# An adapter and LoRA kernel: x of the first two batches loaded in halves, and three more early chunks multiplied in high and low parts

## The chip, the cores and the metric

The kernel runs on one core of one Trainium2 chip. The metric is the device time of one execution in microseconds (us). Its engines are TensorE (PE, matmuls; PEld is its weight load), VectorE (DVE), ScalarE (ACT), GpSimd (POOL) and SyncE (SP), which here only issues transfers. ACTq and SPq are the instruction queues from which an engine issues transfers.

## The reference

Eight batches of x, each of 128 rows by 512 columns. Each batch picks one of 16 adapters (512 by 512) by its id; the result then goes through a base layer and a routed LoRA of 8 experts of rank 16:

```python
y = einsum('bij,bkj->bik', x, weight[adapter_ids])
q = y[:, 107:127].mean(axis=1)
routing = softmax(q @ router_W.T + router_b)
base = y @ W.T + b
t = einsum('bsd,erd->bser', y, A)
lora = einsum('bser,eor,be->bso', t, B, routing) * 2
out = x + base + lora
```

All data is float32.

## The kernel before

The contraction of 512 is cut into four chunks of 128 (C = 4; HALF = 2 chunks). For a batch, y gathers in one PSUM bank over four chunks: x's chunk (128 by 128) is the stationary operand, the adapter's chunk (128 by 512) the moving one. y is then copied to SBUF by ScalarE (copy_y, L265), transposed by TensorE (transpose_y, L544; for batches 4 to 7 VectorE's turn, L406, and transfers do this), and two batches together, a pair g, are multiplied with A and W (products, L552) and with the routed B (lora, L569). VectorE finishes the output (finish, L443) with the bias and x, and SyncE stores it.

A product is made in one of two ways. Raw (y_raw, L511) multiplies the float32 operands as they are; the trace shows two passes for one chunk. Split makes three matmuls of type float32r out of one: ScalarE casts an operand to its high part (hi_...), VectorE subtracts that from the operand to get the low part (lo_...), and TensorE adds high by high, high by low and low by high. Before, batches 0 and 2 are all raw, batch 1 is raw in chunks 0 and 1 and split in chunks 2 and 3 (y1_split, L520, fed by hi_x1, L289, and hi_wc1, L293, and by lo_x1, L380, and lo_wc1, L385), and batches 3 to 7 are split (y_split, L531, fed by hi_x, hi_wc, lo_x, lo_wc).

The order of work is written out by hand, one instruction list for each engine, with semaphores between them. An engine takes its list strictly in order, so an instruction that waits holds all behind it. SyncE issues the loads in the order in which they are listed (L198 to L217): the two halves of adapter 0, x of batch 1, the halves of adapter 1, x of batch 2, and so on; the halves of an adapter are 512 KB each, x of a batch 256 KB. x of batch 0 alone is issued by ScalarE (L311), before its first cast. Adapters are addressed by ids that SyncE reads first (L179).

TensorE's list (L582 to L659) begins with 11 matmuls on zeros, then batch 0, chunks 0 and 1 of batch 1, the transposes of batch 0, chunks 2 and 3 of batch 1, and batch 2 with the transposes of batch 1 after its first chunk. Later the pairs' products alternate with the batches to come. VectorE's list (L449 to L505) ends in a loop over pairs g = 1, 2, 3: the router's parts, half 0 of adapter 2g + 3, the turn of batch 2g + 2, half 1 of that adapter, logits, routing, the low part of t, the next turn, x and adapter 2g + 4, the low parts of yT, and the outputs.

Of the kernel before, what the change touches and what calls it, by code (L numbers as in the profile page):

```python
# [5 lines left out]
P = 128  # L6
# [9 lines left out]
CONSTS = 44  # L16


def adapter_lora_kernel(nc, xT0, xT, ids, wcT, rest0, rest1, rest2, rest3, out):


    _, _, _, C, S = xT.shape
    ALONE = xT0.shape[0]
    PAIRS = xT.shape[0] + ALONE // 2
    B = 2 * PAIRS
    D = C * P
# [7 lines left out]
    RAW = 3  # L34
    WARM_UPS = 11
    ON_PE = 4
    T = 32
    NT = P // T
    assert S == P and C == 4 and B == 8

    with ExitStack() as ctx:
# [6 lines left out]
        def sem(name):  # L48
            return ctx.enter_context(nc.semaphore(name))
# [48 lines left out]
        az_raw = [rest_raw[:, n:n + D] for n in az_at]  # L98
        b_raw = rest_raw[:, FIRST + D:SECOND]

        x_in = [sem(f"x{b}_in") for b in range(ALONE)] + [sem(f"x_pair{g}_in") for g in range(ALONE // 2, PAIRS)]
        wc_in = [[sem(f"wc{b}_in{n}") for n in range(2)] for b in range(B)]
        rest_in = [sem(f"rest{n}_in") for n in range(4)]
        stored = [sem(f"stored{g}") for g in range(PAIRS - 1)]
# [13 lines left out]
        xT_lo_ready = sem("xT_lo_ready")  # L118
        wc_hi_ready = sem("wc_hi_ready")
        wc_lo_ready = sem("wc_lo_ready")  # L120
        x1_hi_ready = sem("x1_hi_ready")
        x1_lo_ready = sem("x1_lo_ready")
        wc1_hi_ready = sem("wc1_hi_ready")
        wc1_lo_ready = sem("wc1_lo_ready")

        y_done = sem("y_done")
        y_copied = sem("y_copied")
# [22 lines left out]
        def flat(t):  # L150
            return t.rearrange("p c s -> p (c s)")
# [4 lines left out]
        def half_of(h):  # L156
            return slice(HALF * h, HALF * (h + 1))

        def x_arrived(b):
            return x_in[b if b < ALONE else b // 2 + ALONE // 2]  # L160

# [15 lines left out]
        @block.sync  # L177
        def _(sp):
            _, a = nc.values_load_multi_w_load_instructions(  # L179
                ids, engines=[mybir.EngineType.SP], min_val=0, max_val=NADAPT - 1,  # L180
                skip_runtime_bounds_check_because="each load of an adapter checks its own address against the table")

            def load_wc(b, h):
                sp.dma_start(wc_raw[:, b, half_of(h), :].rearrange("p c o -> p (c o)"),  # L184
                             wcT[bass.ds(a[b], 1), h].rearrange("a p c o -> (a p) (c o)"))\
                    .then_inc(wc_in[b][h], 16)

            def load_x(b):
                sp.dma_start(flat(xT_raw[:, b]), xT0[b]).then_inc(x_arrived(b), 16)

            def load_x_pair(g):
                sp.dma_start(xT_raw[:, 2 * g:2 * g + 2].rearrange("p b c s -> p (b c s)"),
                             xT[g - ALONE // 2].rearrange("p b c s -> p (b c s)")).then_inc(x_arrived(2 * g), 16)

            def load_rest(n, rest, cols):
                sp.dma_start(rest_raw[:, cols], rest).then_inc(rest_in[n], 16)

            load_wc(0, 0)  # L198
            load_wc(0, 1)
            load_x(1)  # L200
            load_wc(1, 0)
            load_wc(1, 1)
            load_x(2)
            load_wc(2, 0)
            load_rest(0, rest0, slice(0, CONSTS + D))
            load_wc(2, 1)
            load_x(3)
            load_rest(1, rest1, slice(CONSTS + D, FIRST))
            load_rest(2, rest2, slice(FIRST, SECOND))
            load_rest(3, rest3, slice(SECOND, THIRD))  # L210
            load_wc(3, 0)
            load_wc(3, 1)
            for g in range(ALONE // 2, PAIRS):
                load_x_pair(g)
                for b in (2 * g, 2 * g + 1):
                    load_wc(b, 0)
                    load_wc(b, 1)  # L217

            def store(g):
                for c in range(C):  # L220
                    sp.wait_ge(o_ready[c], g + 1)
                sp.dma_start(out[g], o_sb[:, g].rearrange("p c b s -> p c (b s)")).then_inc(stored[g], 16)

            for g in range(1, PAIRS - 1):
                store(g - 1)
                move_blocks(sp, 2 * g + 2)
                move_blocks(sp, 2 * g + 3, range(NT if g == 1 else HALF))
            store(PAIRS - 2)
            for c in range(C):
                sp.wait_ge(o_ready[c], PAIRS)  # L230
                sp.dma_start(out[PAIRS - 1, :, c], o_sb[:, PAIRS - 1, c].rearrange("p b s -> p (b s)"))\
                    .then_inc(last_stored[c], 16)
            for g in range(PAIRS - 1):
                sp.wait_ge(stored[g], 16)
            for c in range(C):
                sp.wait_ge(last_stored[c], 16)
# [17 lines left out]
        def _(act):  # L254
# [31 lines left out]
                    copy(flat(wc_hi[b % 2][:, half_of(h), :]), flat(wc_raw[:, b, half_of(h), :]))\  # L286
                        .then_inc(wc_hi_ready, 1)

            def hi_x1():  # L289
                act.wait_ge(x_arrived(1), 16)  # L290
                copy(flat(xT_hi[1][:, HALF:]), flat(xT_raw[:, 1, HALF:])).then_inc(x1_hi_ready, 1)  # L291

            def hi_wc1(c):  # L293
                act.wait_ge(wc_in[1][1], 16)
                copy(wc_hi[1][:, c, :], wc_raw[:, 1, c, :]).then_inc(wc1_hi_ready, 1)

            def exponent(g):
                act.wait_ge(nmax_ready, g + 1)
# [9 lines left out]
                                         scale=rout[:, i:i + 1]).then_inc(tsT_hi_ready, 1)  # L308

            act.wait_ge(ident_ready, 1)  # L310
            act.dma_start(flat(xT_raw[:, 0]), xT0[0]).then_inc(x_arrived(0), 16)  # L311
            act.wait_ge(warm_ready, 1)
            nc.scalar.activation(junk[:], warm[:, 0:1], ACT.Exp)

            hi_x1()
            copy_y(0, ps_y)
            for c in range(HALF, C):
                hi_wc1(c)
            hi_yT(0)
            copy_y(1, ps_o[3])  # L320
            hi_az(0)
# [33 lines left out]
        def _(dve):  # L355
# [21 lines left out]
                    tt(flat(wc_lo[b % 2][:, part_h, :]), flat(wc_raw[:, b, part_h, :]),  # L377
                       flat(wc_hi[b % 2][:, part_h, :]).bitcast(F32), ALU.subtract).then_inc(wc_lo_ready, 1)

            def lo_x1():  # L380
                dve.wait_ge(x1_hi_ready, 1)
                tt(flat(xT_lo[1][:, HALF:]), flat(xT_raw[:, 1, HALF:]), flat(xT_hi[1][:, HALF:]).bitcast(F32),  # L382
                   ALU.subtract).then_inc(x1_lo_ready, 1)

            def lo_wc1(c):  # L385
                dve.wait_ge(wc1_hi_ready, c - HALF + 1)
                tt(wc_lo[1][:, c, :], wc_raw[:, 1, c, :], wc_hi[1][:, c, :].bitcast(F32), ALU.subtract)\
                    .then_inc(wc1_lo_ready, 1)

            def lo_yT(b):  # L390
                pair, i = b // 2 % 2, b % 2
# [55 lines left out]
                    .then_inc(o_ready[c], 1)  # L447

            nc.vector.memset(warm[:], 0.0).then_inc(warm_ready, 1)  # L449
            lo_x1()  # L450
            for c in range(HALF, C):
                lo_wc1(c)
            lo_yT(0)
            lo_az(0)
            lo_yT(1)
# [12 lines left out]
            lo_wc(3)  # L468
            lo_az(4)
            for b in range(2):  # L470
                dve.wait_ge(x_arrived(b), 16)
            finish(0, 0)
            finish(0, 1)
            lo_x(4)
# [5 lines left out]
            for g in range(1, PAIRS):  # L480
                ahead = 2 * g + 2 < B
                router_parts(g)
                if ahead:
                    lo_wc(2 * g + 3, (0,))
                    turn(2 * g + 2)
                    lo_wc(2 * g + 3, (1,))
                logits(g)
                routing(g)
                lo_tsT(g)
                if ahead:  # L490
                    turn(2 * g + 3)
                if 2 * g + 4 < B:
                    lo_x(2 * g + 4)
                    lo_wc(2 * g + 4)
                if ahead:
                    lo_yT(2 * g + 2)
                for c in range(3):
                    finish(g, c)
                if ahead:
                    lo_yT(2 * g + 3)  # L500
                if 2 * g + 4 < B:
                    lo_x(2 * g + 5)
                if g < PAIRS - 1:
                    finish(g, 3)
# [3 lines left out]
        def _(pe):  # L508
            mm = nc.tensor.matmul

            def y_raw(b, c, bank):  # L511
                if c == 0:
                    pe.wait_ge(x_arrived(b), 16)
                if c % HALF == 0:
                    pe.wait_ge(wc_in[b][c // HALF], 16)
                last = mm(bank[:], xT_raw[:, b, c, :], wc_raw[:, b, c, :], start=(c == 0), stop=(c == C - 1))  # L516
                if c == C - 1:
                    last.then_inc(y_done, 1)

            def y1_split(c, bank):  # L520
                if c == HALF:
                    pe.wait_ge(x1_lo_ready, 1)
                pe.wait_ge(wc1_hi_ready, c - HALF + 1)
                mm(bank[:], xT_hi[1][:, c, :], wc_hi[1][:, c, :], start=False, stop=False)
                mm(bank[:], xT_lo[1][:, c, :], wc_hi[1][:, c, :], start=False, stop=False)
                pe.wait_ge(wc1_lo_ready, c - HALF + 1)
                last = mm(bank[:], xT_hi[1][:, c, :], wc_lo[1][:, c, :], start=False, stop=(c == C - 1))
                if c == C - 1:
                    last.then_inc(y_done, 1)

# [52 lines left out]
            for _ in range(WARM_UPS):  # L583
                mm(ps_l[:], warm[:, 0:P], warm[:], start=True, stop=True)  # L584

            for c in range(C):
                y_raw(0, c, ps_y)
            for c in range(HALF):
                y_raw(1, c, ps_o[3])
            pe.wait_ge(ident_ready, 1)  # L590
            transpose_y(0)
            for c in range(HALF, C):
                y1_split(c, ps_o[3])
            for c in range(C):
                y_raw(2, c, ps_y)
                if c == 0:
# [111 lines left out]
```

## Time and profile before

| | us |
|---|---|
| median of 3 runs | 72.85 (72.40 to 73.01) |
| the profiled execution | 72.17 |
| its span in the trace | 70.5 |
| TensorE busy | 65.9 (94%) |
| VectorE busy | 43.0 (61%) |
| ScalarE busy | 30.5 (43%) |

The profile is of one execution. The span runs from its first to its last instruction. Busy time of TensorE counts overlapping matmuls once; a matmul's record is longer than its step, since matmuls are pipelined, so the step from one record's start to the next is what one costs in a full queue. The granted TensorE clock is 1.0 of full speed in all 40 slices.

### The profile page before, as it was taken

The numbers are of one execution on the slowest core, as the hardware profiler recorded it, in microseconds if no ns is written. First come the engines' busy times: TensorE is split into PE (matmuls) and PEld (weight loads), VectorE is DVE, ScalarE is ACT, GpSimd is POOL, SyncE is SP. The second block draws the span as 40 slices with busy tenths as digits, with TensorE's granted clock in tenths as the row PEclk, the third lists the DMA queues.
The fourth block names the chain that finished last, engine by engine and source line by source line (L and its number), as shares of the span: only waits on it lengthen the run. The fifth ranks groups of instructions, "written<-read, shape, count | busy, mean of one in ns | idle before, by whom it ended". The sixth has DMA issues, their size and how long they took to land.

```text
span 70.5 us, 1142 instructions
## 1 busy us (share of the span) xinstructions
PE 65.9 (94%) x409; PEld 53.9 (76%) x409; DVE 43.0 (61%) x105; ACT 30.5 (43%) x62; POOL 1.2 (2%) x10
## 2 busy tenths in 40 slices
PE   2999989999999999999999999999999999999930
PEld 1332425743999988988988999888699999999920
DVE  1000022938999999779955999699554298250720
ACT  0800055487898993593036997300330330330000
POOL 5000000000000000000000000000000000000000
PEclk9999999999999999999999999999999999999999
DMA  0489999999999999999824014007230600600242
GB/s 0 112 265 384 358 387 409 417 405 414 409 407 412 407 409 405 409 409 402 333 64 104 9 42 107 0 0 298 47 88 19 151 3 9 284 14 0 69 154 74
DMA packets 7062, 15.30 MB, mean 217 GB/s; under 512 B 784, under 2 KB 3344, under 8 KB 7056
## 3 DMA queue, kind: packets, MB, share of 16 engines
q1 hardware_dynamic: 6624, 14.84, 56.2%
q10 hardware_dynamic: 432, 0.39, 2.1%
q8 instruction: 3, 0.05, 0.3%
q14 instruction: 3, 0.02, 0.1%
HBM read 12.08 MB, written 2.10 MB: 201 GB/s over the span
## 4 chain that ended last, share of the span: by engine, by line
PE 81%; DMA 8%; SPq 4%; issue 1%; DVE 1%
PE ps_o L556 32%; PE ps_t L556 8%; PE ps_o L573 8%; DMA wc_raw<-in_wcT_dram 8%; PE ps_y L516 5%; PE ps_y L539 4%; PE ps_y L538 4%; PE ps_y L540 4%; PE ps_yT L538 3%; PE ps_o L516 3%; PE ps_yT L540 3%; PE ps_yT L539 3%; PE ps_yT L549 3%; SPq L179 2%; SPq L184 1%
## 5 line engine op out<-in xcount | busy, mean ns | idle before, releaser
L556 PE MATMUL ps_o<-yT_hi,az_hi 128*128 128x256 f32 x64 | 18.1, 283 | 0.0
L556 PE MATMUL ps_o<-yT_lo,az_hi 128*128 128x256 f32 x64 | 17.8, 279 | 0.0
L556 PE MATMUL ps_o<-yT_hi,az_lo 128*128 128x256 f32 x64 | 17.8, 279 | 0.0
L556 PEld LDWEIGHTS ps_o<-yT_hi,az_hi 128*128 128x128 f32 x64 | 12.0, 188 | 0.1
L556 PEld LDWEIGHTS ps_o<-yT_hi,az_lo 128*128 128x128 f32 x64 | 12.0, 188 | 0.1
L556 PEld LDWEIGHTS ps_o<-yT_lo,az_hi 128*128 128x128 f32 x64 | 12.0, 188 | 0.0
L377 DVE TENSOR_TENSOR wc_lo<-wc_raw,wc_hi 128x1024 fp32r<-128x1024 f32 x10 | 11.9, 1211 | 0.1
L286 ACT CAST wc_hi<-wc_raw 128x1024 fp32r<-128x1024 f32 x10 | 10.0, 1052 | 0.0
L445 DVE SCALAR_TENSOR_TENSOR o_sb<-ps_o,rest_raw,xT_raw 128x256 f32<-128x256 f32 x16 | 7.1, 478 | 3.1 <-PE ps_o L573 3.1
L300 ACT ACTIVATE expd<-logit,nmax 128x8 f32<-128x8 f32 x8 | 2.3, 293 | 12.8 <-DVE nmax L427 12.8
L516 PE MATMUL ps_y<-wc_raw,xT_raw 128*128 128x512 f32 x16 | 7.4, 597 | 0.2 <-DMA wc_raw<-in_wcT_dram 0.2
L584 PE MATMUL ps_l<-warm 128*128 128x512 bf16 x11 | 4.9, 632 | 1.3 <-DVE warm L449 1.3
L516 PEld LDWEIGHTS ps_y<-wc_raw,xT_raw 128*128 128x128 f32 x16 | 2.9, 190 | 3.5 <-issue 2.9
L382 DVE TENSOR_TENSOR xT_lo<-xT_raw,xT_hi 128x256 fp32r<-128x256 f32 x1 | 0.4, 424 | 8.0 <-ACT xT_hi L291 8.0
L539 PE MATMUL ps_y<-wc_lo,xT_hi 128*128 128x512 f32 x12 | 4.7, 391 | 0.0
L538 PE MATMUL ps_y<-wc_hi,xT_hi 128*128 128x512 f32 x12 | 4.7, 391 | 0.0
L540 PE MATMUL ps_y<-wc_hi,xT_lo 128*128 128x512 f32 x12 | 4.7, 389 | 0.0
L399 DVE TENSOR_TENSOR yT_lo<-yT_raw,yT_hi 128x512 fp32r<-128x512 f32 x4 | 2.8, 689 | 3.0 <-ACT yT_hi L276 3.0
L556 PE MATMUL ps_t<-yT_hi,az_hi 128*128 128x256 f32 x16 | 4.6, 285 | 0.0
L573 PE MATMUL ps_o<-tsT_hi,b_hi 128*128 128x256 f32 x16 | 4.6, 284 | 0.0
L276 ACT CAST yT_hi<-yT_raw 128x512 fp32r<-128x512 f32 x4 | 2.5, 624 | 4.7 <-issue 2.9
L573 PE MATMUL ps_o<-tsT_lo,b_hi 128*128 128x256 f32 x16 | 4.5, 283 | 0.0
(71 smaller groups left out, 111.9 us busy)
## 6 DMA issues: line engine op xcount, KB each, us to landing
wc_raw<-in_wcT_dram SPq DMA_DIRECT2D x16, 512.0 KB, 12.1
out_dram<-o_sb SPq DMA_DIRECT2D x3, 512.0 KB, 3.7
rest_raw<-in_rest_dram SPq DMA_DIRECT2D x2, 512.0 KB, 9.5
xT_raw<-in_xT_dram SPq DMA_DIRECT2D x2, 512.0 KB, 14.3
yT_raw<-y_turn SPq DMA_DIRECT2D x14, 64.0 KB, 2.1
xT_raw<-in_xT_dram SPq DMA_DIRECT2D x3, 256.0 KB, 6.7
out_dram<-o_sb SPq DMA_DIRECT2D x4, 128.0 KB, 1.9
rest_raw<-in_rest_dram SPq DMA_DIRECT2D x1, 278.0 KB, 7.6
```

What stands on the lines that cost most here:

```text
L276: copy(yT_hi[b // 2 % 2][:, :, b % 2, :].rearrange("p c (n s) -> p c n s", n=NT), yT_raw[b % 2].rearrange("p n c s -> p c n s")).then_inc( ...
L286: copy(flat(wc_hi[b % 2][:, half_of(h), :]), flat(wc_raw[:, b, half_of(h), :]))\
L377: tt(flat(wc_lo[b % 2][:, part_h, :]), flat(wc_raw[:, b, part_h, :]), flat(wc_hi[b % 2][:, part_h, :]).bitcast(F32), ALU.subtract).then_in ...
L399: tt(yT_lo[pair][:, :, i, :].rearrange("p c (n s) -> p c n s", n=NT), yT_raw[i].rearrange("p n c s -> p c n s"), yT_hi[pair][:, :, i, :].r ...
L445: stt(out=o_sb[:, g, c], in0=ps_o[c][:, 0:N2].rearrange("p (b s) -> p b s", b=2), scalar=bias[:, c:c + 1], in1=xT_raw[:, 2 * g:2 * g + 2, ...
L516: last = mm(bank[:], xT_raw[:, b, c, :], wc_raw[:, b, c, :], start=(c == 0), stop=(c == C - 1))
L538: mm(bank[:], xT_hi[i][:, c, :], wc_hi[i][:, c, :], start=(c == 0), stop=False)
L539: mm(bank[:], xT_hi[i][:, c, :], wc_lo[i][:, c, :], start=False, stop=False)
L540: last = mm(bank[:], xT_lo[i][:, c, :], wc_hi[i][:, c, :], start=False, stop=(c == C - 1))
L556: last = mm(bank[:, 0:N2], stat[:, n, c, :], mov[pair][:, c].rearrange("p b s -> p (b s)"), start=(c == 0 and k == 0), stop=(stop and c == ...
L573: last = mm(ps_o[c][:, 0:N2], stat[:, cols], mov[:].rearrange("p b s -> p (b s)"), start=False, stop=(k == 2))
L584: mm(ps_l[:], warm[:, 0:P], warm[:], start=True, stop=True)
```

## The change

x of batches 0 and 1 is laid out in memory and loaded in halves of two chunks (128 KB each, rows of 1 KB). Half 0 of batch 0 is issued by ScalarE, half 1 by SyncE behind half 0 of adapter 0; the halves of batch 1 go ahead of the halves of adapter 1. Chunks 1 and 3 of batch 0 and chunk 1 of batch 1 are split instead of raw, and the x chunks of batch 1 are split one at a time, each just ahead of its adapter chunk. On VectorE, half 0 of adapter 7 is subtracted in the loop's turn g = 1, ahead of the low part of yT of batch 5, instead of in turn g = 2 ahead of the turn of batch 6. (The new condition at lo_x covers the same turn as before, g = 1.)

```diff
-def adapter_lora_kernel(nc, xT0, xT, ids, wcT, rest0, rest1, rest2, rest3, out):
+def adapter_lora_kernel(nc, xT0, xT1, xT, ids, wcT, rest0, rest1, rest2, rest3, out):
...
+    EARLY = ((0, 1), (0, 3), (1, 1), (1, 2), (1, 3))
...
+            def load_x_half(b, h):
+                sp.dma_start(flat(xT_raw[:, b, half_of(h), :]), xT0[b, h]).then_inc(x_half_in[b][h], 16)
+
             def load_x(b):
-                sp.dma_start(flat(xT_raw[:, b]), xT0[b]).then_inc(x_arrived(b), 16)
+                sp.dma_start(flat(xT_raw[:, b]), xT1[b - 2]).then_inc(x_arrived(b), 16)
...
             load_wc(0, 0)
+            load_x_half(0, 1)
             load_wc(0, 1)
-            load_x(1)
+            load_x_half(1, 0)
             load_wc(1, 0)
+            load_x_half(1, 1)
             load_wc(1, 1)
             load_x(2)
...
-            def hi_x1():
-                act.wait_ge(x_arrived(1), 16)
-                copy(flat(xT_hi[1][:, HALF:]), flat(xT_raw[:, 1, HALF:])).then_inc(x1_hi_ready, 1)
-
-            def hi_wc1(c):
-                act.wait_ge(wc_in[1][1], 16)
-                copy(wc_hi[1][:, c, :], wc_raw[:, 1, c, :]).then_inc(wc1_hi_ready, 1)
+            def hi_x_early(b, c):
+                act.wait_ge(x_half_in[b][c // HALF], 16)
+                copy(xT_hi[b][:, c, :], xT_raw[:, b, c, :]).then_inc(early_x_hi_ready, 1)
+
+            def hi_wc_early(b, c):
+                act.wait_ge(wc_in[b][c // HALF], 16)
+                copy(wc_hi[b][:, c, :], wc_raw[:, b, c, :]).then_inc(early_wc_hi_ready, 1)
...
-            act.dma_start(flat(xT_raw[:, 0]), xT0[0]).then_inc(x_arrived(0), 16)
+            act.dma_start(flat(xT_raw[:, 0, half_of(0), :]), xT0[0, 0]).then_inc(x_half_in[0][0], 16)
...
-            hi_x1()
+            for b, c in EARLY[:3]:
+                hi_x_early(b, c)
+                hi_wc_early(b, c)
             copy_y(0, ps_y)
-            for c in range(HALF, C):
-                hi_wc1(c)
+            for b, c in EARLY[3:]:
+                hi_x_early(b, c)
+                hi_wc_early(b, c)
             hi_yT(0)
...
+            def lo_early(n):
+                b, c = EARLY[n]
+                dve.wait_ge(early_x_hi_ready, n + 1)
+                tt(xT_lo[b][:, c, :], xT_raw[:, b, c, :], xT_hi[b][:, c, :].bitcast(F32), ALU.subtract)\
+                    .then_inc(early_x_lo_ready, 1)
+                dve.wait_ge(early_wc_hi_ready, n + 1)
+                tt(wc_lo[b][:, c, :], wc_raw[:, b, c, :], wc_hi[b][:, c, :].bitcast(F32), ALU.subtract)\
+                    .then_inc(early_wc_lo_ready, 1)
...
-            lo_x1()
-            for c in range(HALF, C):
-                lo_wc1(c)
+            for n in range(len(EARLY)):
+                lo_early(n)
             lo_yT(0)
...
             for b in range(2):
-                dve.wait_ge(x_arrived(b), 16)
+                for h in range(2):
+                    dve.wait_ge(x_half_in[b][h], 16)
...
                 if ahead:
-                    lo_wc(2 * g + 3, (0,))
+                    if g == 1:
+                        lo_wc(2 * g + 3, (0,))
                     turn(2 * g + 2)
                     lo_wc(2 * g + 3, (1,))
...
                 for c in range(3):
                     finish(g, c)
+                if 2 * g + 5 == B - 1:
+                    lo_wc(2 * g + 5, (0,))
                 if ahead:
                     lo_yT(2 * g + 3)
-                if 2 * g + 4 < B:
+                if 2 * g + 5 == B - 1:
                     lo_x(2 * g + 5)
...
             def y_raw(b, c, bank):
-                if c == 0:
+                if b < 2 and c % HALF == 0:
+                    pe.wait_ge(x_half_in[b][c // HALF], 16)
+                elif c == 0:
                     pe.wait_ge(x_arrived(b), 16)
...
+            def y_early(b, c, bank):
+                n = EARLY.index((b, c)) + 1
+                pe.wait_ge(early_x_lo_ready, n)
+                pe.wait_ge(early_wc_hi_ready, n)
+                mm(bank[:], xT_hi[b][:, c, :], wc_hi[b][:, c, :], start=False, stop=False)
+                mm(bank[:], xT_lo[b][:, c, :], wc_hi[b][:, c, :], start=False, stop=False)
+                pe.wait_ge(early_wc_lo_ready, n)
+                last = mm(bank[:], xT_hi[b][:, c, :], wc_lo[b][:, c, :], start=False, stop=(c == C - 1))
                 if c == C - 1:
                     last.then_inc(y_done, 1)
...
-            for c in range(C):
-                y_raw(0, c, ps_y)
-            for c in range(HALF):
-                y_raw(1, c, ps_o[3])
+            y_raw(0, 0, ps_y)
+            y_early(0, 1, ps_y)
+            y_raw(0, 2, ps_y)
+            y_early(0, 3, ps_y)
+            y_raw(1, 0, ps_o[3])
+            y_early(1, 1, ps_o[3])
             pe.wait_ge(ident_ready, 1)
             transpose_y(0)
-            for c in range(HALF, C):
-                y1_split(c, ps_o[3])
+            y_early(1, 2, ps_o[3])
+            y_early(1, 3, ps_o[3])
```

On the host the array xT0 holds the halves of x of batches 0 and 1, and xT1 x of batches 2 and 3. The semaphores are renamed and added to match.

## Rows read from the trace of the kernel before

**Rows 1.** The page, busy us, share of the span, instructions.
```profile
PE 65.9 (94%) x409; PEld 53.9 (76%) x409; DVE 43.0 (61%) x105; ACT 30.5 (43%) x62; POOL 1.2 (2%) x10
```

**Rows 2.** Timeline of TensorE: start us, us, engine line op out<-in [idle before].
```profile
6.29 3.67 PE L516 MATMUL ps_y<-wc_raw,xT_raw 128*128 128x512 f32 x8 [0.15 <-DMA wc_raw<-in_wcT_dram]
```

**Rows 3.** The chain of waits in order of time, 9 to 18 us: start, us, what.
```profile
10.15 1.96 PE ps_o L516 x4
12.11 0.44 PE ps_yT L549 x4
...
13.71 0.23 PE ps_o L527
```

**Rows 4.** Who waited for whom: us in total, times, longest us.
```profile
PEld ps_yT L538 <- DVE wc_lo L377: 0.4, 1, 0.4
```

**Rows 5.** Timeline of SyncE, issues of six loads: start us, us.
```profile
3.35 0.33 SPq L184 DMA_DIRECT2D wc_raw<-in_wcT_dram  x1
3.73 0.42 SPq L189 DMA_DIRECT2D xT_raw<-in_xT_dram  x1
4.35 0.33 SPq L184 DMA_DIRECT2D wc_raw<-in_wcT_dram  x1
4.87 0.33 SPq L184 DMA_DIRECT2D wc_raw<-in_wcT_dram  x1
5.24 0.52 SPq L189 DMA_DIRECT2D xT_raw<-in_xT_dram  x1
...
7.07 0.57 SPq L184 DMA_DIRECT2D wc_raw<-in_wcT_dram  x1
```

**Rows 6.** The same six issues, in order: KB, us from issue to landing.
```profile
wc_raw<-in_wcT_dram SPq DMA_DIRECT2D x1, 512.0 KB, 4.2
xT_raw<-in_xT_dram SPq DMA_DIRECT2D x1, 256.0 KB, 5.0
wc_raw<-in_wcT_dram SPq DMA_DIRECT2D x1, 512.0 KB, 5.7
wc_raw<-in_wcT_dram SPq DMA_DIRECT2D x1, 512.0 KB, 6.4
xT_raw<-in_xT_dram SPq DMA_DIRECT2D x1, 256.0 KB, 6.7
...
wc_raw<-in_wcT_dram SPq DMA_DIRECT2D x1, 512.0 KB, 8.2
```

**Rows 7.** Busy times in three stretches; the last columns: clock, DMA share, GB/s.
```profile
3.60:4.00 0.40, 0.40 (x2) 0.15 (x1) 0.00 (x0) 0.00 (x0) 0.00 (x0) 1.00 0.41 118
4.60:6.80 2.20, 2.04 (x6) 0.60 (x5) 0.00 (x0) 0.00 (x0) 0.00 (x0) 1.00 1.00 400
...
69.00:69.50 0.50, 0.00 (x0) 0.00 (x0) 0.00 (x0) 0.00 (x0) 0.00 (x0) 1.00 0.70 246
```

**Rows 8.** Timeline of ScalarE, casts for batch 1.
```profile
8.79 0.40 ACT L291 CAST xT_hi<-xT_raw 128x256 fp32r<-128x256 f32 x1 [5.32 <-DMA xT_raw<-in_xT_dram]
...
11.31 0.62 ACT L295 CAST wc_hi<-wc_raw 128x512 fp32r<-128x512 f32 x1 [0.73 <-DMA wc_raw<-in_wcT_dram]
```

**Rows 9.** Timeline of VectorE, subtractions for batch 1.
```profile
9.23 0.42 DVE L382 TENSOR_TENSOR xT_lo<-xT_raw,xT_hi 128x256 fp32r<-128x256 f32 x1 [8.03 <-ACT xT_hi L291]
11.96 1.29 DVE L387 TENSOR_TENSOR wc_lo<-wc_raw,wc_hi 128x512 fp32r<-128x512 f32 x2 [2.31 <-ACT wc_hi L295]
```

**Rows 10.** Timeline of VectorE in the turns g = 1 and 2 of its loop.
```profile
44.98 0.69 DVE L399 TENSOR_TENSOR yT_lo<-yT_raw,yT_hi 128x512 fp32r<-128x512 f32 x1 [0.69 <-ACT yT_hi L276]
...
48.94 1.18 DVE L377 TENSOR_TENSOR wc_lo<-wc_raw,wc_hi 128x1024 fp32r<-128x1024 f32 x1
```

**Rows 11.** Timeline of TensorE: project_t of pair 2, and batch 7 in split chunks.
```profile
46.84 0.28 PE L556 MATMUL ps_t<-yT_hi,az_hi 128*128 128x256 f32 x1
...
49.76 0.40 PE L540 MATMUL ps_yT<-wc_hi,xT_lo 128*128 128x512 f32 x1
...
50.51 0.39 PE L539 MATMUL ps_yT<-wc_lo,xT_hi 128*128 128x512 f32 x1
```

More of the change, by code:

```diff
@@ L16 @@
 CONSTS = 44
-def adapter_lora_kernel(nc, xT0, xT, ids, wcT, rest0, rest1, rest2, rest3, out):
+def adapter_lora_kernel(nc, xT0, xT1, xT, ids, wcT, rest0, rest1, rest2, rest3, out):
     _, _, _, C, S = xT.shape
-    ALONE = xT0.shape[0]
+    ALONE = 2 + xT1.shape[0]
     PAIRS = xT.shape[0] + ALONE // 2
@@ L99, in adapter_lora_kernel @@
         b_raw = rest_raw[:, FIRST + D:SECOND]
-        x_in = [sem(f"x{b}_in") for b in range(ALONE)] + [sem(f"x_pair{g}_in") for g in range(ALONE // 2, PAIRS)]
+        x_half_in = [[sem(f"x{b}_in{n}") for n in range(2)] for b in range(2)]
+        x_in = [None] * 2 + [sem(f"x{b}_in") for b in range(2, ALONE)] + [sem(f"x_pair{g}_in") for g in range(ALONE // 2, PAIRS)]
         wc_in = [[sem(f"wc{b}_in{n}") for n in range(2)] for b in range(B)]
@@ L120, in adapter_lora_kernel @@
         wc_lo_ready = sem("wc_lo_ready")
[L121 to L124, printed above, removed]
+        early_x_hi_ready = sem("early_x_hi_ready")
+        early_x_lo_ready = sem("early_x_lo_ready")
+        early_wc_hi_ready = sem("early_wc_hi_ready")
+        early_wc_lo_ready = sem("early_wc_lo_ready")
         y_done = sem("y_done")
@@ L378, in lo_wc @@
                        flat(wc_hi[b % 2][:, part_h, :]).bitcast(F32), ALU.subtract).then_inc(wc_lo_ready, 1)
[L380 to L388, printed above, removed]
+            def lo_early(n):
[6 more added lines that the diff above has]
+                    .then_inc(early_wc_lo_ready, 1)
             def lo_yT(b):
@@ L518, in y_raw @@
                     last.then_inc(y_done, 1)
[L520 to L527, printed above, removed]
+            def y_early(b, c, bank):
[6 more added lines that the diff above has]
+                last = mm(bank[:], xT_hi[b][:, c, :], wc_lo[b][:, c, :], start=False, stop=(c == C - 1))
                 if c == C - 1:
@@ L690 @@
     arrays = {
-        "xT0": xT[:4].reshape(4, P, c * s),
+        "xT0": np.ascontiguousarray(xT[:2].reshape(2, P, 2, c // 2 * s).transpose(0, 2, 1, 3)),
+        "xT1": xT[2:4].reshape(2, P, c * s),
         "xT": np.ascontiguousarray(xT[4:].reshape(-1, 2, P, c, s).transpose(0, 2, 1, 3, 4)),
```

## The prediction

> **What bounds the kernel now.** I read the shares of the page first, then the chain of waits in its order of time, then the transfer issues with their landing times, then the engines' timelines around the two places that the change touches. TensorE is busy for 65.9 of 70.5 us, VectorE for 43.0 and ScalarE for 30.5 [rows 1]. The chain leaves TensorE only at the start. Batch 0's eight raw passes run from 6.29 to 9.96 us [rows 2]. TensorE then stands still until 10.15, because the first half of adapter 1, issued at 4.35, lands 5.7 us later, at about 10.0 [rows 3, 5, 6]. From there the chain is TensorE alone: two raw chunks of batch 1 (1.96 us), four transposes (0.44), six split matmuls that end at 13.94, and so on to the last output [rows 3]. The only later stop that the profile names is 0.4 us of weight load behind the low part of an adapter [rows 4]. So the kernel is a TensorE queue hung on one early landing, and a change moves the end by what it does to that queue at 10 to 14 us and at the one later stop.
>
> **TensorE's work, three chunks split.** A raw chunk takes two passes. Eight of them took 3.67 us and four 1.96 [rows 2, 3]: the difference over four is 0.43 a pass, 0.86 a chunk, with 0.25 of drain behind the last. A split chunk takes three matmuls at a step of 0.23, 0.69 a chunk [rows 3]. Each conversion saves 0.17 us of TensorE time, 0.51 in all. Two of the three lie in batch 0, ahead of the wait for adapter 1: they end batch 0 up to 0.34 us earlier and the wait takes it back, worth 0. In batch 0 the low part of chunk 1 comes after a cast (0.62) and a subtraction (0.69) behind the landing, but chunk 0's raw 0.86 and two split matmuls (0.46) cover 1.32 of it; chunk 3 likewise behind chunk 2. Even 0.2 us lost there has batch 0 done before 10.0. The third conversion, batch 1's chunk 1, moves the transposes forward by up to 0.17, if what follows them is ready.
>
> **What follows them.** Batch 1's chunks 2 and 3 need the second half of adapter 1, landed at W = 4.87 + 6.4 = 11.27 [rows 5, 6]. Before, ScalarE began its first cast at 11.31 and VectorE the first subtraction at 11.96, that is W + 0.69 [rows 8, 9]; TensorE was still transposing until 12.55, so nothing waited. x of batch 1 had been split in one piece at 8.79 and 9.23 [rows 8, 9]. Now each x chunk is cast and subtracted beside its adapter chunk. The nearest rows for a 128-wide x chunk are the 256-wide ones (0.40 and 0.42) and the 512-wide ones (0.62 and 0.69): extended down they give 0.29 each, with a step of about 0.2 in a full queue (two 512-wide subtractions take 1.29, a step of 0.60) [rows 8, 9]. VectorE's queue behind W becomes: adapter chunk 2 from W + 0.69, x chunk 3 from W + 1.29, adapter chunk 3 from W + 1.49 until W + 2.18. ScalarE has chunk 3 cast by about W + 1.37, so it doesn't decide. ScalarE must now also cast batch 1's chunk 1 before it copies y of batch 0 (10.00 before); that copy, one cast of 0.62 and its own 0.6 behind the landing at 10.02, ends near 11.2, and the transposes reach TensorE at about 11.8, so this wait is covered. From the end of a subtraction to the matmul that wanted it passed 0.16 us (48.94 + 1.18 = 50.12; the matmul after it at 50.51, one step of 0.23 earlier its own) [rows 10, 11]. Batch 1's last matmul so starts at W + 2.34; its record started at 13.55, W + 2.28 (the chain writes 13.71 for it). If W stood still, the change would cost 0.06 here instead of gaining 0.17.
>
> **W moves.** Half of x of batch 0 leaves ScalarE's own queue and comes third in SyncE's, behind the first half of adapter 0. Before, all of it landed before the adapters' stream had begun: the transfer engines were 41% busy at 118 GB/s between 3.6 and 4.0 us, against 400 GB/s at full share from 4.6 [rows 7]. So the half that leaves buys nothing there, and 131 KB are added to a full stream. For rows of 1 KB the nearest price is the last store, 246 GB/s at a share of 0.70, or 350 GB/s at full share: 0.37 us for a half [rows 7]. Three halves stand where x of batch 1 stood alone. x of batch 2, the same size, landed 0.67 us after the piece ahead of it (5.24 + 6.7 against 11.27); x of batch 1 took 1.18 (3.73 + 5.0 against 3.35 + 4.2) [rows 5, 6]. I take the excess of 0.5 as something that befell that moment and stays: W grows by 3 x 0.37 - 0.67 = 0.44, to 11.71. Bounds: 0 if the added half only fills gaps, 3 x 0.59 - 1.18 = 0.59 if halves go at the slow rate. SyncE issues a load in about 0.33 to 0.52 us and is 5 to 6 us ahead of the landings [rows 5, 6], so two more issues there cost nothing; that lead covers them. The later loads come 0.44 later too: adapter 2's second half lands at 15.3 + 0.44 [rows 5, 6], before its chunk 2 is wanted, some 2.4 us after batch 1's end.
>
> The Trainium skill speaks against such halves: DMA: Bandwidth & Descriptors, Rules for kernel authors, says to coalesce small transfers into large ones, and its section Bandwidth lists 0.95 us for 64 KB and 6.15 for 1 MB. As an estimate between those two, a half costs 1.3 us and W grows by 1.9, which would make the kernel 1.7 us slower. The trace's 256 KB piece at 0.67 us disagrees, as long as the queue is full.
>
> Start of the queue: batch 1 ends 0.06 + 0.44 = **0.50 us later**. The chains that hang on it (copy, transposes, router) shift along with it, and so does everything to the end.
>
> **The later stop.** The subtraction of adapter 7's first half moves on VectorE from ahead of the turn of batch 6 to ahead of the remainder of yT of batch 5. VectorE waited 0.69 us there, until 44.98, for ScalarE, whose order casts adapter 7 before it [rows 10]; so it is ready. It costs about 1.1 in a full queue, so yT of batch 5 is 0.4 late (46.1, wanted at 46.84 [rows 11]), covered by 0.7. Everything behind its old place comes 0.69 earlier: the second half ends at 49.43 instead of 50.12. TensorE wanted it at 49.99; between the matmuls at 49.76 and 50.51 lie 0.75 us instead of two steps of 0.46 [rows 11]. That stop goes: **-0.29**. Of what is queued behind the moved piece, the fourth output of pair 1 and its store on SyncE come 0.4 later; nothing on the chain waits for them, and the moves of batch 6's blocks behind them wait for the turn, which is earlier. Next late there would be yT of batch 5.
>
> **Sum.** +0.50 - 0.29 = **+0.21 us**. The profiled execution took 72.17 (70.5 of span and 1.7 around it), so 72.38 for such a one; it is 0.68 below the median of 72.85, against which I forecast 73.06.
>
> **Rivals.**
> *The stream is not later.* The added 131 KB fill gaps (the full stream reached 400 GB/s only from 4.6), and the slow 0.5 us around x of batch 1 vanish. Then W is 11.27 or less, and TensorE's own work decides: -0.17 - 0.29 = -0.46, down to 72.4. For it speaks the unexplained 1.18; against it the full share.
> *The conversions count in full.* -0.51 - 0.29 = -0.80, 72.05. This needs the first half of adapter 1 to land 0.3 us earlier, and the same bytes stand before it, with two 1 KB pieces for one of 2 KB.
> *Each small load costs a fixed time (slower).* If the 0.5 us excess of x of batch 1 belongs to a transfer and not to that moment, each half takes 0.87, W grows by 3 x 0.87 - 1.18 = 1.43 and the sum is +1.20, 74.05. Its place is the stream of 6 to 12 us, and it decides from W = 12.2 on. Against it: x of batch 2 paid no such thing. The skill's figures above are this rival's kin.
> *The later stop stays or changes place.* +0.50, 73.35.
>
> **Chances.** Forecast 0.50; later stop stays 0.12; stream not later 0.20; conversions in full 0.06; fixed cost 0.12. A measurement of this kernel can tell about 1%, 0.73 us, from no change. The first three are within it but for their edges: same 0.80, faster 0.08, slower 0.12. The range takes the not-later case with its low edge and the stop that stays, with 0.2 us for the spread of medians: 72.3 to 73.6.
>
> **What would show it.** The cast of adapter 1's chunk 2 starts at about 11.75 instead of 11.31, VectorE runs without a gap from 12.4 to the end of batch 1's chunk 3, TensorE shows waits of 0.2 to 0.3 us on the low parts in batch 1, and batch 1 ends near 14.45 on the chain. No weight load waits near 50 us. TensorE's idle time between batches 0 and 1 is longer. A cast at 11.3 or before, or at 12.2 or after, would make the forecast wrong, and so would a new wait of TensorE behind yT of batch 5.

## The result, and the profile of the changed kernel

| | before | changed |
|---|---|---|
| median, 14 runs each | 72.59 us (72.20 to 73.98) | 73.19 us (72.91 to 73.83) |
| ratio to before (95% interval) | | 1.0103 (1.0075 to 1.0131) |
| profiled execution's span | 70.5 us | 71.5 us |

The ratio leaves out executions more than 1.5% above the fastest of their kernel, as do all ratios below.

The change made the kernel 0.75 us slower (1.03% of 72.59), just at the edge of what I had called no change. The forecast was 73.06, 0.21 more than before: the absolute time was missed by 0.13, but the difference is over three times the forecast one. The absolute time came out closer because the median of three runs from which I started, 72.85, was itself 0.26 above that of fourteen. The profiled execution of before (72.17) also lay 0.42 below its own median, while that of the changed kernel lay at its own; the difference of the two spans, 1.0, is therefore larger than that of the medians.

The page of the changed kernel, parts 1 and 2, busy us and share of the span, and DMA share and rate in 40 slices of 1.79 us:

```profile
PE 65.9 (92%) x412; PEld 54.5 (76%) x412; DVE 45.8 (64%) x112; ACT 32.8 (46%) x69; POOL 1.2 (2%) x10
...
DMA  0288999999999999999744123102630600600142
GB/s 0 73 269 254 293 393 415 410 396 408 408 413 408 410 403 415 408 399 408 316 167 106 41 50 72 39 0 124 232 89 0 147 9 0 280 14 0 65 155 73
```

The last row for the kernel before, in slices of 1.76 us:

```profile
GB/s 0 112 265 384 358 387 409 417 405 414 409 407 412 407 409 405 409 409 402 333 64 104 9 42 107 0 0 298 47 88 19 151 3 9 284 14 0 69 154 74
```

TensorE is as busy as before in us [rows 1] and the span is longer: it waits. The fourth and fifth slices of the transfer rate, 254 and 293 GB/s from 5.4 to 8.9 us, lie below the 393 and more that follow at once, and below the 384 and 358 of the kernel before.

The chain of waits of the changed kernel in order of time (start us, us, what), to be held against [rows 3]:

```profile
3.83 5.47 DMA wc_raw<-in_wcT_dram
9.30 0.14 issue
9.44 1.10 PE ps_y L530 x2
...
11.22 0.94 PE ps_o L530 x2
...
12.87 0.44 PE ps_yT L563 x4
...
13.84 0.24 PE ps_o L539
14.07 0.44 PE ps_o L541
...
14.98 0.32 PE ps_o L541
15.31 0.86 PE ps_y L530 x2
```

The chain now starts at another transfer. Before, TensorE waited for the first half of adapter 1. Now it waits for the second half of adapter 0, issued at 3.83 and landed at 9.30, where the one of before was issued at 3.35 and landed 4.2 later, at 7.55 [rows 5, 6]. Batch 1 ends at 15.31, where the chain passes to batch 2. In the kernel before that piece was

```profile
13.94 0.86 PE ps_y L516 x2
```

so batch 1 ends **1.37 us later**.

SyncE's issues in the changed kernel:

```profile
2.75 0.40 SPq L186 DMA_DIRECT2D wc_raw<-in_wcT_dram  x1
3.21 0.42 SPq L191 DMA_DIRECT2D xT_raw<-in_xT_dram  x1
3.83 0.34 SPq L186 DMA_DIRECT2D wc_raw<-in_wcT_dram  x1
4.21 0.43 SPq L191 DMA_DIRECT2D xT_raw<-in_xT_dram  x1
...
5.82 0.61 SPq L186 DMA_DIRECT2D wc_raw<-in_wcT_dram  x1
```

and, for the last three of these lines, size and us from issue to landing:

```profile
wc_raw<-in_wcT_dram SPq DMA_DIRECT2D x1, 512.0 KB, 5.5
xT_raw<-in_xT_dram SPq DMA_DIRECT2D x1, 128.0 KB, 5.4
...
wc_raw<-in_wcT_dram SPq DMA_DIRECT2D x1, 512.0 KB, 6.8
```

The last one is the second half of adapter 1: W = 5.82 + 6.8 = 12.6, against 11.27 before [rows 5, 6]. The first half of x of batch 1 landed at 9.6, only 0.3 behind adapter 0: from there the stream ran at its normal step. The delay arose in adapter 0's second half: it was 1.7 us there and 1.3 at W.

The trace marks the landing of a load in sixteen parts, and the kernel waits for all of them. Those of adapter 0's second half came between 7.18 and 7.58 us before, and between 7.58 and 9.30 in the changed kernel. The first part is 0.4 us later and the last 1.7: the load landed unevenly, and was not late as a whole.

ScalarE and VectorE around W in the changed kernel, to be held against [rows 8, 9]:

```profile
12.60 0.62 ACT L302 CAST wc_hi<-wc_raw 128x512 fp32r<-128x512 f32 x1 [0.35 <-DMA wc_raw<-in_wcT_dram]
13.13 0.29 ACT L298 CAST xT_hi<-xT_raw 128x128 fp32r<-128x128 f32 x1
```

```profile
13.26 0.69 DVE L396 TENSOR_TENSOR wc_lo<-wc_raw,wc_hi 128x512 fp32r<-128x512 f32 x1 [0.68 <-ACT wc_hi L302]
13.87 0.28 DVE L393 TENSOR_TENSOR xT_lo<-xT_raw,xT_hi 128x128 fp32r<-128x128 f32 x1
14.07 0.68 DVE L396 TENSOR_TENSOR wc_lo<-wc_raw,wc_hi 128x512 fp32r<-128x512 f32 x1
```

VectorE runs adapter chunk 2, x chunk 3 and adapter chunk 3 in one row, and TensorE waits for it twice, as its weight loads show:

```profile
14.00 0.19 PEld L541 LDWEIGHTS ps_o<-wc_lo,xT_hi 128*128 128x128 f32 x1 [0.37 <-DVE wc_lo L396]
...
14.81 0.19 PEld L541 LDWEIGHTS ps_o<-wc_lo,xT_hi 128*128 128x128 f32 x1 [0.27 <-DVE wc_lo L396]
```

At batch 7, TensorE in the changed kernel, to be held against [rows 11]:

```profile
51.09 0.39 PE L554 MATMUL ps_yT<-wc_hi,xT_lo 128*128 128x512 f32 x1
...
51.55 0.39 PE L553 MATMUL ps_yT<-wc_lo,xT_hi 128*128 128x512 f32 x1
```

These two steps, from adapter 7's first half into its second, take 0.46 us where they took 0.75. The subtraction that moved, and the last one of adapter 7, on VectorE (against [rows 10]):

```profile
45.62 1.22 DVE L387 TENSOR_TENSOR wc_lo<-wc_raw,wc_hi 128x1024 fp32r<-128x1024 f32 x1
46.75 0.69 DVE L408 TENSOR_TENSOR yT_lo<-yT_raw,yT_hi 128x512 fp32r<-128x512 f32 x1
...
49.58 1.18 DVE L387 TENSOR_TENSOR wc_lo<-wc_raw,wc_hi 128x1024 fp32r<-128x1024 f32 x1
```

Ahead of this place (project_t of pair 2, against [rows 11]) and behind it (the first product after batch 7), TensorE in the changed kernel:

```profile
48.29 0.28 PE L570 MATMUL ps_t<-yT_hi,az_hi 128*128 128x256 f32 x1
...
52.68 0.28 PE L570 MATMUL ps_o<-yT_hi,az_hi 128*128 128x256 f32 x1
```

and the second of them in the kernel before:

```profile
51.66 0.28 PE L556 MATMUL ps_o<-yT_hi,az_hi 128*128 128x256 f32 x1
```

So the lag of TensorE behind before was 1.45 us (48.29 against 46.84) and is 1.0 from there to the end. The moved subtraction gave 0.4.

### The profile page after: what moved, and what is told of

Its sections match the earlier page's. It is cut to its first block, busy times and chain, and to the rows that moved or that the text cites. A ratio compares the mean times of both kernels' runs of the same rounds, so it can differ in the third digit from the quotient of the medians.

```text
span 71.5 us, 1170 instructions
## 1 busy us (share of the span) xinstructions
PE 65.9 (92%) x412; PEld 54.5 (76%) x412; DVE 45.8 (64%) x112; ACT 32.8 (46%) x69; POOL 1.2 (2%) x10
## 4 chain that ended last, share of the span: by engine, by line
PE 83%; DMA 8%; SPq 4%; issue 1%; DVE 1%
PE ps_o L570 32%; PE ps_t L570 8%; PE ps_o L587 8%; DMA wc_raw<-in_wcT_dram 8%; PE ps_y L530 6%; PE ps_y L552 4%; PE ps_y L553 4%; PE ps_y L554 4%; PE ps_yT L552 3%; PE ps_yT L553 3%; PE ps_yT L554 3%; PE ps_yT L563 2%; SPq L181 2%; PE ps_o L541 1%; PE ps_o L538 1%; PE ps_o L530 1%
## 5 line engine op out<-in xcount | busy, mean ns | idle before, releaser
L307 ACT ACTIVATE expd<-logit,nmax 128x8 f32<-128x8 f32 x8 | 2.3, 293 | 12.6 <-DVE nmax L436 12.6
L396 DVE TENSOR_TENSOR wc_lo<-wc_raw,wc_hi 128x512 fp32r<-128x512 f32 x5 | 3.5, 691 | 6.2 <-ACT wc_hi L302 6.2
L530 PE MATMUL ps_y<-wc_raw,xT_raw 128*128 128x512 f32 x12 | 6.1, 618 | 1.3 <-DMA wc_raw<-in_wcT_dram 1.2
L302 ACT CAST wc_hi<-wc_raw 128x512 fp32r<-128x512 f32 x5 | 3.1, 618 | 5.7 <-DMA wc_raw<-in_wcT_dram 5.7
L530 PEld LDWEIGHTS ps_y<-wc_raw,xT_raw 128*128 128x128 f32 x12 | 2.2, 206 | 3.6 <-issue 3.6
```

The costliest lines, as they stand in the source:

```text
L302: copy(wc_hi[b][:, c, :], wc_raw[:, b, c, :]).then_inc(early_wc_hi_ready, 1)
L396: tt(wc_lo[b][:, c, :], wc_raw[:, b, c, :], wc_hi[b][:, c, :].bitcast(F32), ALU.subtract)\
```

## The experiments

All landings below are from one profile of each kernel, while a ratio is from 3 to 11 of its executions; a profile can lie well off its kernel's median. Two theories at first. *Landing* (A): all that was lost was lost in the landings, and the split chunks cost next to nothing. *Splits* (B): TensorE's waits for low parts cost it. All ratios are to the kernel before, run beside them.

**1. The moved subtraction alone**

```diff
                 if ahead:
-                    lo_wc(2 * g + 3, (0,))
+                    if g == 1:
+                        lo_wc(2 * g + 3, (0,))
                     turn(2 * g + 2)
...
+                if 2 * g + 5 == B - 1:
+                    lo_wc(2 * g + 5, (0,))
                 if ahead:
                     lo_yT(2 * g + 3)
```

> The kernel before with one part of the change: the subtraction of adapter 7's first half moved ahead of the low part of yT of batch 5. Theory A (landing: the changed kernel lost 1.4 us to late landings at its start and won 0.4 at batch 7): 0.3 to 0.45 us faster than before, batch 7's twelve matmuls in 2.8 us instead of 3.13. Rival B (the end of the queue was shorter in the changed kernel for another reason): no difference.

Ratio 0.9977 (0.9936 to 1.0017), too wide to tell 0.4 us from nothing. The trace shows it: in this execution SyncE's first load was issued 0.72 us later than in the profile of before (3.48), batch 1 ended 0.61 later (14.55), and the span was only 0.2 longer (70.7). Batch 7 ran without the stop, in 2.84 us instead of 3.13. The 0.4 is shown in the trace and not by the times.

**2. The splits without the half loads**

```diff
             load_wc(0, 0)
-            load_x_half(0, 1)
             load_wc(0, 1)
-            load_x_half(1, 0)
+            load_x_whole(1)
             load_wc(1, 0)
-            load_x_half(1, 1)
             load_wc(1, 1)
```

with x of batch 0 whole on ScalarE, as before.

> The changed kernel with x of batches 0 and 1 loaded whole, as before; the three more split chunks and the moved subtraction stay. Theory A (landing): adapter 1's second half lands at about 11.3 us, batch 1 ends within 0.1 us of before, and the kernel is 0.3 to 0.5 us faster than before. Rival B (the splits themselves cost, through TensorE's waits on low parts in batches 0 and 1): it stays 0.4 us or more above before.

Ratio 0.9996 (0.9956 to 1.0036). Rival B is out: with whole loads the changed kernel's loss is gone. The gain of 0.3 us that A expected isn't shown either. The landing and the end of batch 1 came out later than A wanted (11.8 and 15.6 us), but that is in an execution of 73.48, 0.9 above this kernel's median of 72.61; the last section says what held it up.

**3. The half loads without the splits**

```diff
             load_wc(0, 0)
+            load_x_half(0, 1)
             load_wc(0, 1)
-            load_x(1)
+            load_x_half(1, 0)
             load_wc(1, 0)
+            load_x_half(1, 1)
             load_wc(1, 1)
```

in the kernel before, with all products as they were.

> The kernel before with only the loads of the change: x of batches 0 and 1 in halves, second half of batch 0 on SyncE. All products as before. Theory A (landing): adapter 0's second half lands near 9.3 and adapter 1's near 12.5, and the kernel is 0.9 to 1.2 us slower than before, more than the changed kernel. Rival B (the splits cost): 0 to 0.3 us slower.

Ratio 1.0157 (1.0100 to 1.0213), 1.1 us. A holds: the loads alone cost as much as the whole change or more (the single value is higher, the intervals overlap).

**4. Both halves of x of batch 0 on ScalarE**

```diff
             load_wc(0, 0)
-            load_x_half(0, 1)
             load_wc(0, 1)
...
             act.dma_start(flat(xT_raw[:, 0, half_of(0), :]), xT0[0, 0]).then_inc(x_half_in[0][0], 16)
+            act.dma_start(flat(xT_raw[:, 0, half_of(1), :]), xT0[0, 1]).then_inc(x_half_in[0][1], 16)
```

> The changed kernel with both halves of x of batch 0 issued by ScalarE, back to back; x of batch 1 stays in halves on SyncE. If the piece put between the halves of adapter 0 is what makes the stream late (theory A1), adapter 0's second half lands near 7.6 and the kernel is 0.2 to 0.5 us faster than before. If loads of 1 KB rows make it late wherever they stand (rival C), adapter 1's second half lands after 12 and it is 0.3 us or more slower than before.

Ratio 1.0045 (1.0000 to 1.0091), between the two. The landings favour the place: adapter 0's second half landed 5.4 us after the first issue and adapter 1's 8.9. But theory A1 had wanted 4.8 and a faster kernel, and neither came. Seven of the twelve executions took 72.49 to 72.81 us and five 73.27 to 73.68, and the profile is one of those five.

**5. The half of batch 0 behind both halves of adapter 0**

```diff
             load_wc(0, 0)
-            load_x_half(0, 1)
             load_wc(0, 1)
+            load_x_half(0, 1)
             load_x_half(1, 0)
```

> The changed kernel with the second half of x of batch 0 issued behind both halves of adapter 0 instead of between them. All bytes as in the changed kernel. If the place between the halves is what upsets the stream (theory P), adapter 1's second half lands about 9.3 us after the issue of the first load (it was 9.8 in the changed kernel, 8.5 before), and the kernel is 0.4 to 0.7 us faster than the changed one, at 0 to 0.4 us over before. If it is only the bytes or the 1 KB rows, wherever they stand (theory Q), it lands 9.8 us after it and the time stays 0.6 us or more over before.

Ratio 0.9944 (0.9915 to 0.9972), 1.6% below the changed kernel, from two lines in another order. That is more than theory P (the place) expected, so I ran it once more:

> The five-split kernel with the second half of x of batch 0 behind adapter 0, once more, to see whether 0.994 of before holds. If it does: 0.991 to 0.998. If that was the luck of nine runs: about 1.000 to 1.003, which is what its landing of 9.35 us after the first issue would give.

Ratio 0.9977 (0.9945 to 1.0009), where the two intervals overlap; both lie below that of the changed kernel. Theory Q (bytes and row sizes alone), which wanted 9.8 and 0.6 us over before, is out. One thing doesn't fit. In both profiles adapter 1's second half landed about 0.8 us later than before, batch 1 ended 0.9 later (14.89 and 14.81 us), and the spans are longer than before's (71.1 and 71.0), yet by the runs these kernels are not slower than before. The profiled executions took 72.80 and 72.72, above the medians of 72.29 and 72.61, so part of that lateness may belong to these two executions alone.

**6 and 7. Other pieces in that place**, in the kernel of experiment 4

```diff
             load_wc(0, 0)
+            load_x_half(1, 0)
             load_wc(0, 1)
-            load_x_half(1, 0)
             load_wc(1, 0)
```

> As the kernel with both halves of x of batch 0 on ScalarE, but the first half of x of batch 1 (128 KB, 1 KB rows) goes between the halves of adapter 0. Not one byte more ahead of adapter 1 than there. Theory P (place): adapter 1's second half lands 9.6 us or more after the first issue, against 8.9 there, and the time rises by 0.5 us or more over that kernel. Theory Q (bytes): 8.9, and no difference.

Ratio 1.0092 (1.0056 to 1.0128).

```diff
             load_wc(0, 0)
+            load_x(2)
             load_wc(0, 1)
...
             load_wc(1, 1)
-            load_x(2)
             load_wc(2, 0)
```

> As the kernel with both halves of x of batch 0 on ScalarE, but x of batch 2 (256 KB, 2 KB rows) goes between the halves of adapter 0. Bytes alone add 0.67 us ahead of adapter 1: theory Q and a theory that only 1 KB rows upset the stream both give a landing 9.6 us after the first issue. Theory P (any piece there costs about 0.9 more than its bytes) gives 10.3 or more.

Ratio 1.0120 (1.0078 to 1.0162). Adapter 1's second half landed 9.5 us after the first issue in the one (P wanted 9.6, Q 8.9) and 10.2 in the other (P 10.3, Q 9.6). The place it is, and not the 1 KB rows, as far as single profiles tell; the ratio of the first still overlaps with that of experiment 4.

**8. Nothing in that place, only a late issue**, in the kernel of experiment 4

```diff
             load_wc(0, 0)
+            sp.wait_ge(x_half_in[0][0], 16)
             load_wc(0, 1)
```

> As the kernel with both halves of x of batch 0 on ScalarE, nothing between the halves of adapter 0, but SyncE waits for the first half of x of batch 0 before it issues adapter 0's second half: that issue goes from 3.2 to about 3.85 us, as late as in the changed kernel, with no piece ahead of it. If the late issue is what costs (theory L), adapter 0's second half lands 6.2 us or more after the first issue and the time is 1.009 of before or more. If the piece itself is (theory P), it lands 4.8 to 5.7 us after it and the time stays as without the wait, 1.000 to 1.006 of before.

Ratio 1.0111 (1.0069 to 1.0153). P falls too, as the piece isn't needed: SyncE issued adapter 0's second half at 3.92, 1.05 us after the first, and it landed 5.4 us later. The transfer engines in three stretches of this kernel (last columns: clock, DMA share, GB/s):

```profile
5.00:6.00 1.00, 0.41 (x2) 0.00 (x0) 0.00 (x0) 0.00 (x0) 0.00 (x0) 1.00 0.94 348
6.00:7.00 1.00, 0.57 (x2) 0.30 (x2) 0.04 (x1) 0.69 (x2) 0.00 (x0) 1.00 0.99 267
7.00:8.00 1.00, 1.00 (x5) 0.56 (x3) 0.86 (x2) 0.13 (x1) 0.00 (x0) 1.00 0.87 253
```

and in the second kernel of experiment 10, with no wait and 0.59 us between the two issues:

```profile
5.00:6.00 1.00, 1.00 (x3) 0.15 (x1) 0.00 (x0) 0.00 (x0) 0.00 (x0) 1.00 0.96 393
6.00:7.00 1.00, 0.73 (x3) 0.38 (x3) 0.00 (x0) 0.00 (x0) 0.00 (x0) 1.00 1.04 429
7.00:8.00 1.00, 1.00 (x4) 0.33 (x3) 0.00 (x0) 0.00 (x0) 0.00 (x0) 1.00 1.02 333
```

Between 6 and 7 us the late one moves 267 GB/s at a busy share of 0.99, the other 429 at 1.04: its packets take longer. Against experiment 4, the same kernel without the wait, which moved 414 GB/s in that stretch, the ratios' intervals overlap, but all six executions (72.95 to 73.66) lie above experiment 4's larger group (72.49 to 72.81). The landing is 6.5 us after the first issue against 5.4. Its first part came at 7.32 us, against 7.38 there, and its last at 9.31 against 8.16: uneven again.

**9. The late issue in the kernel before**

```diff
             load_wc(0, 0)
+            sp.wait_ge(x_arrived(0), 16)
             load_wc(0, 1)
```

> The kernel before with one wait added on SyncE: x of batch 0 has to land (about 4.15 us) before adapter 0's second half is issued, so that issue goes from 3.35 to about 4.2 us; no load and no product is changed. Theory L (the late issue alone makes the stream uneven): adapter 0's second half lands 6.2 us or more after the first issue instead of 4.8, adapter 1's second half 9.5 or more instead of 8.5, and the kernel is 0.7 to 1.5 us slower than before. Rival (the late issue cost only where x comes in halves of 1 KB rows): 0 to 0.3 us slower, since the first half of the adapter keeps the transfer engines busy until 5.6.

Ratio 1.0121 (1.0025 to 1.0216), some 0.9 us, though with only three executions in it, from one wait on a queue that was still at work on the first half. The same three stretches:

```profile
5.00:6.00 1.00, 1.00 (x3) 0.15 (x1) 0.00 (x0) 0.00 (x0) 0.00 (x0) 1.00 0.82 246
6.00:7.00 1.00, 0.72 (x3) 0.38 (x3) 0.00 (x0) 0.00 (x0) 0.00 (x0) 1.00 0.81 217
7.00:8.00 1.00, 1.00 (x4) 0.38 (x2) 0.00 (x0) 0.00 (x0) 0.00 (x0) 1.00 0.99 315
```

Here the share is below 1 as well, so some transfer engines stood idle. The landings came a little short of what I expected, 6.1 for 6.2 and 9.3 for 9.5. Adapter 0's second half was issued 0.9 us later and landed 1.3 later. Adapter 1's was issued 0.9 later too and landed 0.8 later, so what this kernel lost can also be read as a lateness passed on; that the landing loses more than the issue rests on adapter 0's.

**10. Versions meant to be faster.** One with the moved subtraction and chunk 1 of batch 1 split, loads as before:

```diff
-            for c in range(HALF):
-                y_raw(1, c, ps_o[3])
+            y_raw(1, 0, ps_o[3])
+            y1_split(1, ps_o[3])
```

> The kernel before with the moved subtraction of adapter 7 and one more split chunk, chunk 1 of batch 1; all loads as before, x of batch 1 split in one piece (chunks 1 to 3). By the steps of 0.43 a raw pass and 0.23 a split matmul the third conversion gives 0.17 us, since adapter 1's first half is waited for before it; with the 0.4 of the moved subtraction 0.4 to 0.6 us faster than before (ratio 0.992 to 0.995). Rival: the cast of chunk 1 stands ahead of the copy of y of batch 0 on ScalarE and delays the transposes; then no more than the 0.4.

Ratio 0.9954 (0.9930 to 0.9978), 0.33 us faster than before, a little short of the 0.4 to 0.6 expected. And the same with x of batch 0 in halves, the second one behind adapter 0 (the one with the stretches above):

```diff
             load_wc(0, 0)
             load_wc(0, 1)
+            sp.dma_start(flat(xT_raw[:, 0, half_of(1), :]), xT0[1]).then_inc(x0_in1, 16)
             load_x(1)
```

> The moved subtraction and the one split chunk of batch 1, with x of batch 0 in halves, the second one behind both halves of adapter 0, and x of batch 1 whole behind that. If putting it behind is what made the five-split kernel with that order fast (0.994 of before), it should do as well here: 0.990 to 0.996. If the two further splits of batch 0 did that, 1.000 or more, since 128 KB more stand ahead of adapter 1 (0.37 us) than with x of batch 0 whole.

Ratio 0.9946 (0.9915 to 0.9978), 0.39 us faster than before. The two can't be told apart; both beat before and the changed kernel.

All kernels together, sorted by the gap between the issues of adapter 0's two halves (in us, from issue and landing rows of one profile each, counted from the first issue; the landings are good to 0.1):

| kernel | gap | adapter 0, half 2 | adapter 1, half 2 | ratio |
|---|---|---|---|---|
| before | 0.59 | 4.8 | 8.5 | 1 |
| 1 | 0.59 | 4.6 | 8.4 | 0.998 |
| 2 | 0.59 | 5.7 | 8.9 | 1.000 |
| 4 | 0.59 | 5.4 | 8.9 | 1.0045 |
| 5, again | 0.59 | 5.5, 4.7 | 9.4, 9.3 | 0.994, 0.998 |
| 10, both | 0.59 | 5.1, 4.8 | 8.8, 8.6 | 0.995, 0.995 |
| changed | 1.08 | 6.6 | 9.9 | 1.010 |
| 3 | 1.07 | 6.8 | 10.2 | 1.016 |
| 6 | 1.08 | 6.2 | 9.5 | 1.009 |
| 7 | 1.08 | 6.9 | 10.2 | 1.012 |
| 8 | 1.05 | 6.5 | 9.7 | 1.011 |
| 9 | 1.48 | 6.1 | 9.3 | 1.012 |

The two groups don't overlap in the landing of adapter 0's second half, nor do the ratios, taken as single values. In that of adapter 1's they do (9.4 in 5, 9.3 in 9). Why the second large load lands so unevenly when it is issued about one microsecond after the first, though the first keeps the transfer engines busy until about 5.6, is not shown by these traces, and stays open.

## Why the prediction was right and wrong

**The queue behind W: right.** The forecast put batch 1's last matmul at W + 2.34. The trace marks W at 12.58, so that is 14.92; its record started at 14.82. By the chain batch 1 ended at W + 2.73, against W + 2.65 before. A 128-wide cast took 0.29 (0.29 forecast), a subtraction 0.28 (0.29), VectorE had no gap there, and the waits on low parts were 0.37 and 0.27 (0.2 to 0.3). So the 0.06 of the sum held, within 0.02.

**W moves: the step that failed, in its size.** I took 0.37 us for the added half and 0.44 for W in all. W moved by 1.3. By the prediction's own sign, a cast at 12.2 or after, this term was wrong: the cast started at 12.60. That the total still came within 0.13 us of 73.06 is luck: the start lost 0.87 more than forecast, the later stop gave 0.14 more, and the 72.85 I added to was 0.26 too high. The price was right for what a half costs once the stream runs: the halves of x of batch 1 landed 0.31 and 0.36 behind the pieces ahead of them (0.37 forecast). What I called free was what cost: "two more issues there cost nothing; that lead covers them". One of them moved the issue of adapter 0's second half from 3.35 to 3.83, and experiments 8 and 9 show such a loss with that lateness alone, with no piece and no byte added. Against experiment 4 the late issue moved adapter 1's second half by some 0.8 us; with the 0.44 for the bytes that makes 1.2 of the 1.3. That split is an estimate: four profiles with the loads of the kernel before (before, 1, 2 and the first of 10) spread from 8.4 to 8.9 us for this landing. The lead of 5 to 6 us, which I had read from the rows, is the time from issue to landing with many loads queued; when the second large load was issued, SyncE's queue held a single large one, issued 0.59 us before (1.08 in the changed kernel). And TensorE's longer idle time, which I expected between batches 0 and 1, came in the middle of batch 0 (1.21 us), as it was adapter 0 that landed late.

**The rival of a fixed cost: the right side, the wrong mechanism.** It forecast 74.05, from an excess that each half would pay, and its growth of W, 1.43, is nearer to the 1.3 measured than my 0.44. But the first half of x of batch 1 landed 0.3 us behind the piece ahead of it and paid nothing. The excess of 0.5 around x of batch 1 in the trace of before remains unexplained. It is no chance of that one execution: with the same loads x of batch 1 took 1.20 us in experiment 1 and 1.22 in the first of 10, against 1.18 before, and only in 2 was it 0.68, with adapter 0's second half later there.

**The later stop goes: right, and somewhat more.** 0.29 forecast, 0.43 found: 0.29 between the two halves of batch 7 as forecast, and 0.13 ahead of its first matmul, which had also waited for the subtraction of the first half (0.27 us behind the logits before, 0.14 now). That the low part of yT of batch 5 would be covered held: it started at 46.75, 1.5 us ahead of project_t.

**The conversions of batch 0 are worth nothing: not contradicted.** They couldn't show it in the changed kernel, where TensorE waited 1.2 us in the middle of batch 0. With whole loads, experiment 2 is no faster than experiment 1. The third conversion's 0.17 fits with 0.9954 against 0.9977, inside the intervals, and in that trace the transposes start 1.80 us after batch 1's first pass instead of 1.96.

**The sum.** +0.50 - 0.29 became +1.37 - 0.43 in the traces, +1.0 with a few hundredths between, and +0.75 by the runs.

## What to carry to other kernels

A stream's second large load has little queued ahead of it, so what delays its issue can count in full and more: here 0.46 us of later issue, with no piece added, became 1.1 us of later landing (8 against 4, one profile each). Put small pieces behind the large loads that start the stream (experiment 5), and read a moved transfer's price from the place it goes to, not from the same transfer in a full stream.

## What the runs showed of the hardware that was not expected

The late issue itself: with 1.05 us or more between the first two large loads, the second landed 6.1 to 6.9 us after the first issue in six profiles; with 0.59, it landed 4.6 to 5.7 us after it in eight. The rate at 6 to 7 us doesn't separate the two: it was 191 GB/s in the changed kernel, 267 in experiment 8 and 217 in 9, but 351, 351 and 393 in 3, 6 and 7, against 341 to 429 with the early issue. What grows, with a small overlap, is the time between the first and the last of the sixteen parts of that landing: 1.2 to 2.1 us, against 0.2 to 1.3.

TensorE at half its rate until 10.6 us, though the profile's clock column says 1.00. The chain of waits of the kernel of experiment 2:

```profile
7.21 2.05 PE ps_y L529 x2
9.26 0.43 PE ps_y L537
...
10.11 0.43 PE ps_y L540
...
11.48 0.23 PE ps_y L537
```

From 7.2 to 10.5 us a split matmul of 512 columns took 0.43 us, the pace of the 1.2 GHz level, and 0.23 later, that of 2.4 GHz. The clock had not fallen there; it had not risen yet. In all profiles the matmuls on zeros start at 1.26 us and step by 0.43 at first. The trace's first clock record, of full speed, begins at 4.3 to 7.1 us in eleven profiles, at 10.6 in that of experiment 2 and at 10.7 in that of 4; experiment 5's has none. The column counts the time ahead of that record as full speed, also in the kernel before, where the record begins at 6.2. In 2 and 4 TensorE had stood still for 1.1 and 0.8 us after the matmuls on zeros, as the loads had come late, but those of experiments 1, 6 and 8 stood still for 1.2, 1.6 and 1.0 and ran at full pace. So the idle time alone doesn't tell which follows.

It costs some 1.1 us: in experiments 2 and 4 batch 1 ended 3.8 us behind W, against 2.7 in the changed kernel. Both this and the first load's issue may spread the runs of one kernel; the latter lay between 2.75 and 3.48 us in these profiles.
